# Moving four shared expert units behind the sorted ones, and the first batch's gather and sums into the expert stage

## What is computed

```python
x = x + 0.5 * moe(layernorm(x))        # expert layer, first time
x = x + attention(layernorm(x))        # one head of 256
x = x + 0.5 * moe(layernorm(x))        # expert layer, second time
x = x + 0.5 * fp6_linear(layernorm(x))
x = x + heads_attention(layernorm(x))  # 16 heads
x = x + 0.5 * fp6_linear(layernorm(x))

def moe(x):    # 16 experts in 4 groups: the 2 best groups, then the 4 best experts in them; F = 128
    g = silu(x @ w1_e); u = x @ w3_e
    routed = sum over e of ((g * u) @ w2_e) * combine[:, e]
    shared = (silu(x @ w1_s) * (x @ w3_s)) @ w2_s          # two experts that all rows use
    return routed + shared
```

## Time and profile before

| | us |
|---|---|
| median of three runs | 2498.21 (2496.28 to 2503.7) |
| the profiled execution | 2505.04, its span 2503.0 |
| TensorE busy | 2125.0, 85% of the span |
| VectorE busy | 1520.2, 61% |
| ScalarE busy | 970.8, 39% |
| GpSimd busy | 317.7, 13% |
| mean granted TensorE clock | 0.913 |

### The profile page before, as it was taken

How to read it: one execution, slowest core, us unless ns; L and a number is a source line. 1 busy time by engine, 2 the same in 40 slices (tenths; PEclk the granted TensorE clock), 3 DMA queues, 4 the chain that set the end, 5 groups by cost and what they waited for, 6 DMA issues and landing times.

```text
span 2503.0 us, 38627 instructions
## 1 busy us (share of the span) xinstructions
PE 2125.0 (85%) x12842; PEld 1588.6 (63%) x12842; DVE 1520.2 (61%) x4411; ACT 970.8 (39%) x1961; POOL 317.7 (13%) x298
## 2 busy tenths in 40 slices
PE   4689999957899966899999456678998998999957
PEld 2578888846788945788888335434454554554446
DVE  7843443356555578443344597676876776778277
ACT  4222322322333352222332244235555556555632
POOL 4410000031000044100000342311001002000000
PEclk8899999978999988999999767679999999999966
DMA  8110101120000041101100220423322422332001
GB/s 262 58 57 27 31 27 31 29 66 24 1 1 1 1 118 59 52 27 31 31 27 29 79 61 26 77 45 59 49 31 52 68 36 53 59 46 28 2 26 51
DMA packets 84035, 114.83 MB, mean 46 GB/s; under 512 B 12212, under 2 KB 73816, under 8 KB 80728
## 3 DMA queue, kind: packets, MB, share of 16 engines
q1 hardware_dynamic: 77416, 94.80, 17.3%
q0 software_dynamic: 6432, 17.57, 2.2%
HBM read 69.16 MB, written 43.17 MB: 45 GB/s over the span
## 4 chain that ended last, share of the span: by engine, by line
PE 62%; DVE 25%; ACT 5%; issue 4%; DMA 2%; POOL 2%; DVEq 0%; ACTq 0%; SPq 0%; POOLq 0%
PE psum L775 10%; PE psum L777 10%; PE psum L776 10%; PE psum L126 5%; PE psum L2289 4%; PE psum L128 4%; PE psum L127 4%; DVE mt L2177 4%; PE psum L2268 3%; PE psum L862 3%; DVE m L2165 2%; PE psum L2248 2%; DVE m L2174 2%; DVE stats L160 2%; PE psum L2272 1%
## 5 line engine op out<-in xcount | busy, mean ns | idle before, releaser
L2128 ACT ACTIVATE pt<-psum 128x512 f32<-128x512 f32 (+3 forms) x768 | 333.6, 493 | 275.3 <-DVE psum L2203 180.5
L740 DVE SCALAR_TENSOR_TENSOR h<-psum,xg,sg 128x128 f32<-128x128 f32 x592 | 166.7, 344 | 415.5 <-PE psum L862 415.5
L556 ACT ACTIVATE sg<-psum 128x512 f32<-128x512 f32 x180 | 107.5, 597 | 543.7 <-PE psum L777 543.7
L775 PE MATMUL psum<-w_hi,xt_hi 128*128 (+1 forms) x720 | 286.0, 397 | 17.9 <-DVE xt_lo L705 17.2
L776 PE MATMUL psum<-w_lo,xt_hi 128*128 (+1 forms) x720 | 284.2, 395 | 0.0
L777 PE MATMUL psum<-w_hi,xt_lo 128*128 (+1 forms) x720 | 283.7, 394 | 0.0
L2248 PE MATMUL psum<-ks,qs 96*128 96x512 bf16 (+3 forms) x768 | 235.8, 347 | 34.0 <-DVE m L2165 8.8
L2268 PE MATMUL psum<-qs,ks 99*128 99x512 bf16 (+3 forms) x768 | 239.3, 334 | 24.4 <-ACT pt L2128 18.8
L775 PE MATMUL psum<-w_hi,ht_hi 128*128 (+1 forms) x720 | 217.1, 302 | 0.2
L2177 DVE CUSTOM_DVE_ANT_0 mt<-psum,band_q 128x256 bf16<-128x256 f32 (+1 forms) x512 | 204.6, 400 | 18.2 <-PE psum L2248 7.9
L2272 PE MATMUL psum<-band,ident_r 128*128 128x256 f32 (+1 forms) x864 | 215.0, 337 | 0.0
(11 more groups left out here) (283 smaller groups left out, 4399.7 us busy)
## 6 DMA issues: line engine op xcount, KB each, us to landing
xg<-w_dram SPq DMA_DIRECT2D x54, 256.0 KB, 3.3
qk_scr<-parts SPq DMA_DIRECT2D x32, 384.0 KB, 2.5
qs<-qk_scr SPq DMA_DIRECT2D x96, 128.0 KB, 7.1
ks<-qk_scr SPq DMA_DIRECT2D x96, 128.0 KB, 7.8
xg<-rows_in SPq DMA_DIRECT2D x74, 132.0 KB, 2.2
rows_out<-yb SPq DMA_DIRECT2D x74, 128.0 KB, 1.7
x<-x_dram SPq DMA_DIRECT2D x4, 1024.0 KB, 8.6
out_dram<-x SPq DMA_DIRECT2D x4, 1024.0 KB, 4.5
```

What stands on the lines that cost most here:

```text
L740: ins = dve.scalar_tensor_tensor(out=h[i % 2][:, e, :], in0=u[:, e, :], scalar=xg[j % XSLOT][:, at:at + 1], in1=sg[i % 2][:, e, :], op0=AL ...
L775: pe.matmul(out, a[0], b[0], start=first, stop=False)
L2128: act.activation(pt[n % NPT][:, 0:q1 - q0], st_bank(n)[:, 0:q1 - q0], ACT.Exp).then_inc(*exped.up())
```

## The change

Four of the sixteen shared units (`LATE = 4`, units 12 to 15 of old) now run behind the 74 sorted ones: `NS0 = 12` shared units stand ahead. `fetch` 0 to 3 and `turn_x` 0 and 1 move up with that, to just ahead of unit 11. The two `turn` pairs of the late units move too: one into the sorted stretch (after its fourth unit), one behind the first late unit. Their transposed rows go to the buffers of `xt` that are free then.

In the same stage and beside the late units POOL gathers the 8 tiles of the first batch (`gather` 0 to 7, once every `rows_out` write has landed), and DVE adds them to `X` and takes mean and variance, one tile at a time (`combine` 0 to 3 behind unit 89's tokens, 4 to 7 one unit later). The attention and the linear stage lose these gathers and sums; the attention's list now begins with `weights`. Both expert layers use the same code.

```diff
+        LATE = 4
+        NS0, NSORT = NSH - LATE, 2 * SORTED
+        NUNIT = NSH + NSORT
...
-            for c in range(NCH - 2):
+            for c in range(4):
                 order += (turns(NCH + c) if c else []) + unit(2 * c + 4)
-                if c < 4:
-                    order += [("again", c + 4), ("scatter", c + 4)]
-                order += unit(2 * c + 5) if c < NCH - 3 else []
-            order += [("fetch", j) for j in range(XSLOT)] + [("turn_x", 0), ("turn_x", 1)] + unit(NSH - 1)
-            for i in range(NSH, NUNIT + 2):
+                order += [("again", c + 4), ("scatter", c + 4)]
+                order += unit(2 * c + 5) if c < 3 else []
+            order += [("fetch", j) for j in range(XSLOT)] + [("turn_x", 0), ("turn_x", 1)] + unit(NS0 - 1)
+            rows = [[("gather", t) for t in range(BT)], []] + [[("combine", t) for t in range(n, n + BT // 2)]
+                                                               for n in range(0, BT, BT // 2)]
+            for i in range(NS0, NUNIT + 2):
                 order += unit(i)
...
+                if i == NS0 + 3:
+                    order += turns(NCH + 4)
+                if i == NS0 + NSORT:
+                    order += turns(NCH + 5)
+                if i > NS0 + NSORT:
+                    order += rows.pop(0) if rows else []
...
                         elif kind == "down" and not in_sorted(i):
                             if i == 0:
                                 pe.wait_ge(*w_lo(4))
+                            elif i == NS0 + NSORT:
+                                pe.wait_ge(*y_ok(SORTED))
                             else:
-                                pe.wait_ge(*shared_x(i))
+                                pe.wait_ge(*shared_x(shared_of(i)))
...
# wide_order: the attention stage
-            order = [("gather", t) for t in range(BT)] + [("weights", 0)] + [("gather", t) for t in range(BT, NT)]
-            order += [("combine", c) for c in range(BT // 2)] + [("variance", 0), ("rsqrt", 0)]
+            order = [("weights", 0)] + [("gather", t) for t in range(BT, NT)] + [("variance", 0), ("rsqrt", 0)]
...
# linear_order: rows()
-                yield [("gather", t) for t in range(CT)]
+                yield [("gather", t) for t in range(BT, BT + CT)]
                 for b in range(BATCH):
-                    for c in range(b * BT // TILES, (b + 1) * BT // TILES):
+                    for c in range(b * BT // TILES, (b + 1) * BT // TILES) if b else ():
```

More of the change, by code:

```diff
@@ L241, in __init__, with moe_order @@
                     e.wait_ge(*made(3))
-        def moe_order(fresh, sums):
+        def moe_order(fresh):
             def unit(i):
@@ L249, in unit @@
                     out.append(("turn_h", i - 1))
-                j = (i - NSH) // 2 + 2
-                if i >= NSH and (i - NSH) % 2 == 0 and j < SORTED:
+                j = (i - NS0) // 2 + 2
+                if i >= NS0 and (i - NS0) % 2 == 0 and j < SORTED:
                     out.append(("turn_x", j))
@@ L296, in moe_order, with moe @@
             order += unit(3) + [("table", 0)]
-            for c in range(NCH - 2):
+            for c in range(4):
                 order += (turns(NCH + c) if c else []) + unit(2 * c + 4)
-                if c < 4:
-                    order += [("again", c + 4), ("scatter", c + 4)]
-                order += unit(2 * c + 5) if c < NCH - 3 else []
-            order += [("fetch", j) for j in range(XSLOT)] + [("turn_x", 0), ("turn_x", 1)] + unit(NSH - 1)
-            for i in range(NSH, NUNIT + 2):
+                order += [("again", c + 4), ("scatter", c + 4)]
[4 more added lines that the diff above has]
+            for i in range(NS0, NUNIT + 2):
                 order += unit(i)
-                j = (i - NSH) // 2 + XSLOT
-                if (i - NSH) % 2 and j < SORTED:
+                j = (i - NS0) // 2 + XSLOT
+                if (i - NS0) % 2 and j < SORTED:
                     order.append(("fetch", j))
[L308 to L314, removed]
+                if i == NS0 + 3:
[4 more added lines that the diff above has]
+                    order += rows.pop(0) if rows else []
+            return order + sum(rows, [])
+        def moe(fresh, routing):
+            order = moe_order(fresh)
             gate_ring = Ring([u for u in order if u[0] in ("logit", "back") or u[0] == "turn" and u[1] < KD * NCH],
@@ L475, in on_sp @@
                                 *S.dma(f"rows_in{i % XSLOT}").up())
-                        elif kind == "down" and i >= NSH and tile_of(i)[1]:
+                        elif kind == "down" and in_sorted(i) and tile_of(i)[1]:
                             j = tile_of(i)[0]
@@ L751, in on_dve @@
                                               x_part(i, 0).bitcast(F32), ALU.subtract).then_inc(*x_lo.up())
-                        elif kind == "down" and i < NSH:
+                        elif kind == "down" and not in_sorted(i):
                             dve.wait_ge(*down(i + 1))
@@ L818, in on_pe @@
                             ins.then_inc(*prefix.up())
-                        elif kind == "up" and i < NSH:
+                        elif kind == "up" and not in_sorted(i):
                             c, places, _ = shared_tiles(i)
@@ L970, in attention_wide, with slot_in @@
             SLOTS_IN = 12
+            def slot_in(t):
+                return (t - BT) % SLOTS_IN
             def landed(t):
-                return S.dma(f"gathered{t // 2 % (SLOTS_IN // 2)}")
+                return S.dma(f"gathered{slot_in(t) // 2}")
             def nth(kind, i):
```

67 lines of the change are left out of this document (38 added, 29 removed).

## The result

The changed kernel took 2507.6 us (median of 9 runs, 2504.0 to 2512.4) beside 2498.2 us (9 runs) before: a ratio of 1.0041, 95% interval 1.0026 to 1.0057, 9.4 us slower. The traces explain what the medians leave open, so they come first.

The account below looks back on a forecast made before the run. PE was taken as full in the sorted units, with gains only in the seams, paced by DVE. +1.9 us in the first layer and +8.2 in the second gave +10.1 on 2498.2, so 2508.3 us; range 2498 to 2520.

Parts of the forecast that it names:

- The front: Before the first sorted unit: PE waits 10.0 us for `fetch` 0, then loses 2.3 us to low clock; sorted start 165.0.
- The rival in which the fetch does not hold PE: At `turn_x` 0: rows already there when unit 10 ends, −14.5 us in all, 2483.7 us; chance 0.07.
- The tail: End of the expert stage: eight gathers and sums follow the late units; next stage starts at 545.8, 13.9 us later.
- the slow-gather rival: Expert stage's tail: gathers take 2.3 us instead of 1.3 beside DVE, +18 us in all, 2516 us; chance 0.10.
- The attention: Attention's start: without first-batch gathers and sums, scores begin 12.0 us sooner after the stage's start, bounds 9 and 14.
- The linear stage: Linear stage's start: four pairs of sums leave DVE, but a gather wait remains; 5.7 us back, bounds 2 and 10.
- The sum: Both layers: first 13.9 − 12.0 = +1.9 us, second 13.9 − 5.7 = +8.2 us, together +10.1 us.
- the seams give more: Attention and linear stages: they give back 14 and 10 us, so +4 us, 2502 us; chance 0.13.
- The last step: Whole kernel: 2515.1 us on the profiled execution, less its 6.8 us over the median, gives 2508.3 us.
- Slower by over 0.3%: Whole kernel: the changed kernel is more than 0.3% slower than before; chance 0.66.

Follow-up runs that it names:

- second comparison: The changed kernel, unaltered, measured again against the kernel before: 2504.1 us (12 runs) against 2504.1 us (29 runs), ratio 1.0002.
- the kernel with extra matmuls: Changed kernel plus matmuls with unread results, 38 before each layer's first `turn_x`, 40 before the attention's first scores: 2501.3 us, 0.9992 against the kernel before.
- the early second pass: Changed kernel with row weights and scatter ahead of the units of their round in the last two shared rounds: 0.9989 against the kernel before.
- two late units: Changed kernel with `LATE = 2` instead of 4, so fourteen shared units ahead of the sorted ones: 2495.6 us, 0.9967 against the kernel before.
- the units alone: Changed kernel keeping the four late units, with first-batch gathers and sums put back in attention and linear stages: 1.0054 against the kernel before.
- spread sums: Changed kernel with earlier second row pass, last shared unit between fetch and `turn_x`, sums grouped two, three, three: 2485.2 and 2487.1 us, 0.9948 and 0.9933 against before.
- the one with all extra matmuls: Changed kernel with earlier row pass, moved last shared unit, sums grouped 2-3-3, and 9, 3 and 40 unread matmuls in PE's waits: 2482.1 us, 0.9911 against before.
- the sums alone: Changed kernel with `LATE = 0`, all shared units ahead, first-batch gathers and sums behind the last sorted unit: 1.0030 against the kernel before.

## Why the prediction was right or wrong

The predicted time, 2508.3 us, is 0.7 us from the first median. That is partly luck: the predicted sum was +10.1 us, the traces give +4.3 and +3.5, and the second comparison found no difference.

- **The front held.** Wait 10.0 predicted, 9.88 and 9.86 measured; first sorted unit 165.0 and 164.67. Clock 2.3 predicted, 1.9 and 1.7 by the kernel with extra matmuls. The rival in which the fetch does not hold PE fell in both layers; the early second pass shows what would move those rows.
- **The tail held, step by step.** Predicted and measured: gathers 527.0 and 526.62, first sum 534.8 and 534.17, last sum's end 545.4 and 545.34. A tile took 1.14 us, not 1.05, and the start 0.6 earlier set that off. The eight gathers kept a step of 1.25 us, so the slow-gather rival fell; only the last two ran beside DVE's sums here (one took 1.16 us instead of 0.95), but with two late units five did, and kept both the step and 0.95 us.
- **The attention was short behind its scores.** The start came as told: first sum of the second batch 12.1 us into the stage predicted, 12.4 measured; 10.9 of the 12.0 us were back at the scores: the wait of 2.04 us for the first projection, of which the prediction let half go, stayed whole (561.79). Part of what came back is a collision that the prediction took along without naming it. Before, one pair of the first batch's sums lasted 4.95 us and not 0.76, beside POOL's splits of the weights (541.78 to 545.48):

```profile
541.17 4.95 DVE L1075 SCALAR_TENSOR_TENSOR x<-gathered,x 128x256 f32<-128x256 f32 x2 [0.69 <-DMA gathered<-rows_out,rstd]
```

The step "from there DVE runs the same 12 pairs, so the scores begin 12.0 us sooner" ended the account at the scores. Behind them 3.2 us more came back, so layer 1 was −0.4, not +1.9. From the scores to the second norm behind them (L185) it took 30.3 us before and 28.2 after: 0.8 in the first low stretch, 1.2 where the low stretch near 611 is missing. Is that the change's doing? The stretch stands in both profiles without the moved sums (before, and the units alone) and is missing in nine of the eleven with them; it stands in the other two, the second profile with spread sums (0.69) and the one with all extra matmuls (0.66). These counts leave both open, the change and chance; if it is chance, the cost by the milestone is up to 1.2 us more than +4.3.

- **The linear stage was mis-sized: 9.9 back, not 5.7.** The step named the wait behind the weight's split, and it is there (5.96 us); at the first full `amax`, 27.9 us into the stage where 26.6 was predicted and 29.0 stood before, only 1.1 us is back. The gain comes later: the fourth full `amax` (1493.92, before 1489.00) is 9.3 us nearer to the stage's start, and between the third and the fourth the kernel before still has four pairs of sums, the changed one none. The whole stage up to POOL's add, before and after (windows):

```profile
1404.89:1521.54 116.65, 51.74 (x186) 35.02 (x187) 103.79 (x247) 42.24 (x84) 52.93 (x52) 0.62 0.26 71
```

```profile
1419.06:1525.81 106.75, 50.15 (x186) 33.49 (x187) 92.34 (x223) 42.35 (x84) 40.66 (x44) 0.60 0.24 67
```

DVE is busy 11.5 us less and stands idle 1.6 us more, which gives the 9.9. The four pairs account for 7.3 of the 11.5, as predicted; the other 4.1 are operations that lasted longer before, the term that the prediction left out of its sum and put only into its upper bound, 10. The largest are L1471 with its 3.57 us and a pair of sums beside a POOL operation:

```profile
1476.58 2.50 DVE L1429 SCALAR_TENSOR_TENSOR x<-xn,x 128x256 f32<-128x256 f32 x2
1477.51 1.28 POOL L1654 TENSOR_TENSOR band<-band_full,band 128x512 fp32r<-128x512 f32 x1
```

The Trainium skill (SBUF — State Buffer, "SBUF: two separate sides") states that a DVE operation with two SBUF inputs and a GpSimd operation that reads SBUF exclude each other for the whole instruction. In length the rows agree: a sum took 2.22 us at 1437.60 and 2.19 in the kernel with the sums alone, each ending 0.3 us behind the POOL operation beside it, and 0.42 without such company. Which of the two had started first the rows do not tell, since the stretched sums' rows begin 0.6 us ahead of POOL's. In the second profile of the changed kernel the sum of 2.22 us took 0.43 (1437.88). The prediction cited that section for gathers only, and did not apply it to the sums.

- **The sum.** With these two sizes the prediction's own working gives +4, which was its rival "the seams give more" (2502 us, 0.13). By the traces that rival is what happened. The last step, setting off the profiled execution's 6.8 us against the median, treated what follows the linear stage as equal; it differs by 5.5 us between two executions of the changed kernel, and by 13.3 us (969.2 and 982.5) between the two profiles with spread sums.
- **Slower by over 0.3%** is true of the first comparison and not of the second; the traces put it near +4 us, under that bound. What makes the medians of one kernel differ between comparisons (2507.6 and 2504.1 for the changed one) stays open. Of the readings, one was loose: the 2.1 to 4.1 us of the earlier trace rows hold for scatters and fetches together; the 2.3 us taken from them fit (issue at 155.14, rows used at 157.42).

## What to carry to other kernels

Work that is moved away from a place may have been the cover of something slow there; ask what finishes behind it before asking what the work gains elsewhere, and move only as much as the cover allows: two units gained 7 us, four lost 4. When sums or copies are moved off a busy engine, count what they were colliding with, and follow the account past the first wait. Where runs scatter more than the effect, read a milestone behind the last touched step in several profiles, and not the median alone.

## What the runs showed of the hardware

A PE that was given matmuls in its waits, whose results nobody reads, kept its clock: 0.69 became 1.00 behind a wait of 9.9 us. The length of the wait does not tell the clock behind it: 2.11 us were followed by 0.57, 2.37 us once by 1.00 and 2.34 us once by 0.54. A sum of two SBUF tensors on DVE took 0.42 us alone and 2.2 us beside one POOL operation of 1.27 us, and the same sum of one kernel took 2.22 us in one profile and 0.43 in another, so one such meeting is worth 1.8 us with no change of the kernel. A gather's issue on POOL took 0.95 us, but 1.96 to 1.98 where it began 0.1 us behind the start of a 1.2 us DVE operation on two SBUF tensors, and it ended 0.8 us behind that operation (before: 1438.14, 1453.26, 1470.86).
